# The causal mask of one-head diagonal banks: from a TensorE product to the instruction that takes the maximum

## The reference

```
scores = einsum('bhqd,bhkd->bhqk', Q, K) / sqrt(16)
scores = where(causal, scores, -100000.0)
A = softmax(scores);  Z = A V
out = sum over heads of Z WO, plus 16 * bO
```

## Time and profile before

| | us |
|---|---|
| median of three runs | 1577.11 |
| the profiled execution | 1581.26 |
| span of its trace, first to last instruction | 1579.5 |
| granted TensorE clock, mean over the span | 0.958 |
| DVE busy in the span | 1029.0 |
| attention's first unit of maxima, about | 565 to 600 |
| its steady steps, about | 600 to 1095 |

### The profile page before, as it was taken

The page is one execution under the profiler, slowest core; times in us unless marked ns, Lnnn a source line. Parts: engine busy times, 40 slices in busy tenths (PEclk is TensorE's granted clock), DMA queues, the critical chain, the costliest instruction groups (busy, mean ns, idle before and its releaser), DMA issues. The chain is left out here.

```text
span 1579.5 us, 32613 instructions
## 1 busy us (share of the span) xinstructions
PE 1429.2 (90%) x10020; PEld 978.9 (62%) x10020; DVE 1029.0 (65%) x2383; ACT 775.6 (49%) x1316; POOL 636.5 (40%) x676
## 2 busy tenths in 40 slices
PE   4899999999968879999999999999598999999997
PEld 3777888888846623443444344443276778888886
DVE  5675536365779678877788687784267564445557
ACT  4313565555125514665566466567362245655530
POOL 3371433766634460222222122222235406176764
PEclk9899999999979968999999999999879999999999
DMA  7741656887316910432224242200131227488873
GB/s 258 231 191 54 195 184 203 264 244 241 87 58 169 239 62 2 69 54 43 42 42 68 34 64 42 42 2 2 41 96 69 97 64 245 154 264 249 245 224 107
DMA packets 159219, 199.06 MB, mean 126 GB/s; under 512 B 18181, under 2 KB 132441, under 8 KB 159065
## 3 DMA queue, kind: packets, MB, share of 16 engines
q1 hardware_dynamic: 140632, 146.67, 34.9%
q0 software_dynamic: 18432, 50.36, 9.7%
HBM read 105.21 MB, written 91.49 MB: 125 GB/s over the span
## 5 line engine op out<-in xcount | busy, mean ns | idle before, releaser
L1576 ACT ACTIVATE attn_prob<-attn_b_ps 128x1024 f32<-128x1024 f32 (+3 forms) x352 | 304.1, 870 | 219.6 <-PE attn_b_ps L1744 217.7
L1622 DVE TENSOR_REDUCE attn_max_a<-attn_a_ps 128x1 f32<-128x512 f32 (+3 forms) x432 | 279.1, 669 | 72.5 <-PE attn_a_ps L1727 40.5
L475 POOL DMA_INDIRECT xs_dram<-ffn_xn,ffn_index x192 | 189.0, 984 | 229.1 <-DVE ffn_index L745 172.8
L1724 PE MATMUL attn_a_ps<-k_rows,q_rows 96*128 96x512 bf16 (+3 forms) x768 | 250.1, 348 | 21.2 <-DVEq L1614 7.5
L489 POOL DMA_INDIRECT ffn_gathered<-ys_dram,ffn_index x192 | 195.8, 1020 | 92.8 <-issue 56.0
L1520 POOL TENSOR_SCALAR_AFFINE_SELECT attn_prob<-attn_prob 128x512 f32<-128x512 f32 x128 | 81.3, 636 | 363.5 <-ACT attn_prob L1576 360.7
L789 DVE TENSOR_TENSOR ffn_xs_lo<-ffn_xt_ps,ffn_xs_hi 128x512 fp32r<-128x512 f32 x144 | 97.7, 679 | 160.1 <-ACT ffn_xs_hi L561 159.6
L1768 PE MATMUL attn_o_ps<-attn_prob,attn_v_now 128*17 128x256 f32 (+1 forms) x2560 | 187.8, 366 | 0.0
L1744 PE MATMUL attn_b_ps<-q_rows,k_rows 98*128 98x512 bf16 (+3 forms) x768 | 186.2, 330 | 0.3 <-ACT attn_prob L1576 0.3
L1724 PEld LDWEIGHTS attn_a_ps<-k_rows,q_rows 96*128 96x128 bf16 x768 | 75.0, 98 | 180.0 <-DVE attn_max_a L1622 103.2
L186 PE MATMUL ffn_gu_ps<-ffn_w_hi,ffn_xs_hi 128*128 x564 | 170.7, 303 | 2.1 <-DVE ffn_xs_lo L789 2.1
(11 more groups left out here) (196 smaller groups left out, 2691.7 us busy)
## 6 DMA issues: line engine op xcount, KB each, us to landing
ffn_xs<-xs_dram SPq DMA_DIRECT2D x138, 256.0 KB, 3.4
ys_dram<-ffn_y SPq DMA_DIRECT2D x138, 256.0 KB, 2.5
xs_dram<-ffn_y SPq DMA_DIRECT2D x16, 768.0 KB, 11.7
qk_parts<-proj_cut SPq DMA_DIRECT2D x32, 384.0 KB, 3.1
k_rows<-qk_parts SPq DMA_DIRECT2D x96, 128.0 KB, 4.5
q_rows<-qk_parts SPq DMA_DIRECT2D x96, 128.0 KB, 6.5
ffn_w_stage<-in_L_ffn_w_dram SPq DMA_DIRECT2D x64, 128.0 KB, 2.4
x_res<-in_L_attn_x_dram SPq DMA_DIRECT2D x4, 1024.0 KB, 8.3
```

Of the source, the lines that this page charges most:

```text
L475: pool.indirect_dma_start(xs_dram[(b + 1) % 2], bass.IndirectOffsetOnAxis(index[:, b, i, k:k + 1], 0), xn[:, b % 2, i, :], None, bounds_ch ...
L1576: act.activation(prob[PROB[kt]][:, h:h + heads, prob_at(kt, kt * P):prob_at(kt, S)], b_ps[:, slot, :].rearrange("p (h t) -> p h t", h=head ...
L1622: dve.tensor_reduce(dst, a_ps[:, bank, 0:heads * keys].rearrange("p (h k) -> p h k", h=heads), AX.X, ALU.max).then_inc(a_free, 1)
L1724: ins = pe.matmul(a_ps[:, bank, i * keys:end], q_rows[q][0:SROWS, h0 + i, qt * P:(qt + 1) * P], k_rows[q][0:SROWS, h0 + i, first:first + k ...
```

## The change

For diagonal banks with one head the mask product is no longer issued on PE. DVE reads the bank together with a wide mask (`mask_wide`, 512 columns of bfloat16, zero except for the triangle in the last 128) in one `tensor_tensor_reduce`: it adds the two, writes the sum to a new SBUF tile `scored` that nothing reads, and keeps the running maximum, which is put into the same place as before. Ahead of it stands a semaphore increment that carries the wait for `a_ready`. The banks with two or four heads are as before.

```diff
+        scored = sb("scored", [P, 2, HALF], BF16)
...
+        mask_qk = mask_wide[:, HALF - P:HALF]
...
             def query_maxima(item, q):
-                qt, first, keys, _, h, heads = item
+                qt, first, keys, diagonal, h, heads = item
                 bank, number = ring.take()
                 dve.wait_ge(a_ready, number + 1)
                 dst = max_b[...] if first else max_a[...]
+                if diagonal and heads == 1:
+                    dve.sem_inc(diagonal_begun, 1)
+                    dve.tensor_tensor_reduce(out=scored[:, bank, 0:keys], in0=a_ps[:, bank, 0:keys], in1=mask_wide[:, HALF - keys:HALF],
+                                             scale=1.0, scalar=NEG, op0=ALU.add, op1=ALU.max, accum_out=dst).then_inc(a_free, 1)
+                    return
                 dve.tensor_reduce(dst, a_ps[...], AX.X, ALU.max).then_inc(a_free, 1)
...
-                                    k_rows[q][0:SROWS, h0 + i, first:first + keys], start=True, stop=not diagonal)
-                    if diagonal:
-                        ins = pe.matmul(a_ps[:, bank, end - P:end], ident_b[:, :], mask_qk[:, :],
+                                    k_rows[q][0:SROWS, h0 + i, first:first + keys], start=True, stop=not (diagonal and heads > 1))
+                    if diagonal and heads > 1:
+                        ins = pe.matmul(a_ps[:, bank, end - P:end], ident_b[:, :], mask_qk,
                                         start=False, stop=True)
...
-            for t in (ident, ident_b, mask_qk):
+            for t in (ident, ident_b, mask_wide):
                 ins = pool.memset(t[:, :], 0.0)
```

More of the change, by code:

```diff
@@ L1306, in _, with attention @@
                 values(c, c % 2)
-def attention(nc, x_res, v_res, ident, ident_b, mask_qk, wo, bo, rows):
+def attention(nc, x_res, v_res, ident, ident_b, mask_wide, wo, bo, rows):
     with ExitStack() as ctx:
@@ L1362, in attention @@
         values_taken = sem("values_taken")
+        diagonal_begun = sem("diagonal_begun")
         max_ready = sem("max_ready")
@@ L1863, in _, with constants @@
             sequence(B - 1, True)
-def constants(nc, ident, ident_b, mask_qk, before_b, ones_b):
+def constants(nc, ident, ident_b, mask_wide, before_b, ones_b):
     with ExitStack() as ctx:
@@ L1884, in _ @@
                                    pattern=[[-1, P]], channel_multiplier=1).then_inc(made, 1)
-            pool.affine_select(out=mask_qk[:, :], in_=mask_qk[:, :], compare_op=ALU.is_ge, fill=NEG, base=0,
+            pool.affine_select(out=mask_wide[:, HALF - P:HALF], in_=mask_wide[:, HALF - P:HALF], compare_op=ALU.is_ge, fill=NEG, base=0,
                                pattern=[[-1, P]], channel_multiplier=1).then_inc(made, 1)
@@ L1903, in program @@
         ident_b = sb("ident_b", [P, P], BF16)
-        mask_qk = sb("mask_qk", [P, P], BF16)
+        mask_wide = sb("mask_wide", [P, HALF], BF16)
         before_b = sb("before_b", [P, P], BF16)
@@ L1908, in program @@
         row_gathered = [ctx.enter_context(nc.semaphore(f"row_gathered{i}")) for i in range(G_RING)]
-        first = constants(nc, ident, ident_b, mask_qk, before_b, ones_b)
+        first = constants(nc, ident, ident_b, mask_wide, before_b, ones_b)
         parts = nc.dram_tensor("qk_parts", [2, 3, D, TOKENS], BF16, kind="Internal").ap()
@@ L1919, in program @@
             norm_ctx.close()
-            attention(nc, x_res, v_res, ident, ident_b, mask_qk, wo, bo, rows)
+            attention(nc, x_res, v_res, ident, ident_b, mask_wide, wo, bo, rows)
         ffn(nc, "ffn2", 1, scattered, row_gathered, gate_t, None, x_res, ident, before_b, ones_b, gate_w, w1, w3, w2, xs_dram, ys_dram, out)
```

## The result

The changed kernel takes 1567.18 us (median of 9 runs, 1560.46 to 1571.9); the kernel before, run beside it, takes 1575.48 (9 runs, 1569.97 to 1580.8). The ratio is 0.9951, with a 95% interval from 0.9932 to 0.9969: 5 to 11 us faster. The forecast was 1566, a gain of 11.

The account below looks back on a forecast made before the run. PE's queue was taken to bound the kernel: -14.2 (masks removed) + 2.9 (PE waiting for DVE) + 0.35 (mask fill) = -11 us, so 1566 against the median 1577.11. Forecast's own range 1560 to 1570; 8-in-10 range 1560 to 1587.

Parts of the forecast that it names:

- What bounds it: Steady attention steps: PE's queue sets the unit's length; 236 mask products at 0.06 us each save at most 14.2 us.
- The main part of the pair: DVE's new two-operand instruction on masked banks: costs what the old reduction did, 688 ns for 512 columns.
- The half-rate rival: DVE's main part streams at half rate: about 80 us lost, 1657 in all; chance 0.04.
- The read, d: DVE's second instruction, putting out the maximum: extra time per masked bank, from 0.03 to 0.29 us, taken as 0.12.
- all rivals that rest on a long read: DVE's read of the maximum is long: Half-hidden, chance 0.28, or slower from d = 0.22 (1586 at 0.30), chance 0.18.
- The wait on its own instruction: DVE, semaphore instruction ahead of the main part: its extra step was put at 0.04 us.
- Where PE waits: Banks b7, b8 and b35: PE waits 0.14 and 0.05 us, 0.19 a unit, 2.9 us in 15 units.
- PE's growing waits: Steady attention steps, list of waits: PE's waits for DVE grow from 3 to about 6 us.
- The start: Kernel start: POOL fills 512 columns of mask instead of 128 and the other engines wait, +0.35 us.
- the first banks: 20 masked banks ahead of the steps: taken as 0 extra; about +1.5 us at d = 0.29.
- Half-hidden: Masked banks b4 to b10, b30 to b35: d 0.15 to 0.28, gain of 8 to loss of 8 us; chance 0.28.
- PE waits for something else anyway: Whole kernel: the change does nothing since PE waits for something else, 1577 us; chance 0.03.

Follow-up runs that it names:

- experiment 1: The kernel before without the mask products of one-head diagonal banks, nothing in their place, DVE unchanged; 1565.19 us, 0.9915 of the kernel before.
- experiments 3: The kernel before with only a semaphore increment, carrying the wait, ahead of the old reductions of one-head diagonal banks; 1580.24 us, 1.0016 of the kernel before.
- 4: The changed kernel with DVE's loop written out and the semaphore increment dropped, the new instruction carrying the wait; 1561.10 us, 0.9890 of the kernel before.
- experiment 5: The changed kernel with DVE's loop written out and the semaphore increment kept; 1568.40 us, 0.9945 of the kernel before.
- 10: The kernel of 4 run again, in a second set of runs; 1561.54 us, 0.9908 of the kernel before.

## Why the prediction was right

The time lies in the forecast's own range, and for the reason forecast: PE's queue gets shorter, and DVE gives nearly all banks back in time. The gain, about 8 us (5 to 11), is at the low end of the 8 to 14 that the forecast named. Two terms of it were mis-sized, in opposite directions, and that they nearly cancel is luck.

**What bounds it: right.** PE's queue sets the unit's length. Taking 16 products out of it shortened the unit by their distance, 0.06 each (0.059 by experiment 1), not by their duration of 229 ns.

**The main part of the pair: right.** Predicted as the old instruction, measured 690 and 556 ns. The half-rate rival is out by this row.

**The read, d: wrong in size.** Taken as 0.12, with 0.03 as the lowest end, below which it lies; it is 0.00 from start to start (0.61 with the read, 0.61 without). I had taken it to start when the main part is over. It starts 0.08 before that, together with the next main part. So all rivals that rest on a long read are out. "VectorE: DVE Perf Modes" of the Trainium skill was weighed there: its section "Two Vector instructions with no wait between them" agrees with these rows (0.61 between starts of instructions that last 0.69). Its section "The DRAIN you can't avoid", which the prediction set against it, itself says that a next instruction that is not held starts earlier, so the two do not disagree here.

**The wait on its own instruction: wrong in size.** Taken as 0.04 more, from the chain in the earlier trace rows; it is 0.15 (0.19 instead of 0.04), shown by experiments 3, 4 and 5. The chain's gap was that of waits which the waiting instruction itself carries, so it was no row for this. In the trace of the change the increment starts at 627.44, 0.04 after b5's product has ended, and the main part 0.15 behind the increment: the wait ends as early as before, and the step from the increment to the next instruction is what costs.

**Where PE waits: right places, near the sizes, for a wrong reason.** Predicted 0.14 at b7 and b8 and 0.05 at b35; measured 0.13 at b7 and 0.10 at b35. The free read and the dear wait nearly cancel, by luck: a bank that is waited for was to be free 0.08 + 0.75 = 0.83 after its product's end, and is free after 0.19 + 0.69 = 0.88; with the wait on the main part it would be 0.04 + 0.69 = 0.73. What I called PE's growing waits (from 3 to 6 us in that view) did not show: PE is idle 0.06 at b7 and 0.03 at b35, too short for that list, and the rest of the loss only takes overlap away.

**The start: POOL right, the first banks not quite.** 0.32 measured for 0.35. Ahead of the steps I took 0 for 20 banks and 0.4 came: a pair of masked banks takes 1.56 (first two rows) instead of 1.50. Its loop gained 0.15 of wait and lost 0.10 of mask, not 0.06: in the kernel before a bank's product runs 0.61 alone, and with its mask until 568.56, 0.71 after its start (last two rows). PE's granted clock is 0.50 in this stretch (560 to 600 after), the lower of its two levels, 1.2 of 2.4 GHz:

```profile
567.94 0.69 DVE L1627 CUSTOM_DVE_ANT_0 attn_scored<-attn_a_ps,mask_wide 128x512 bf16<-128x512 f32 x1 [0.27 <-PE attn_a_ps L1732]
...
569.50 0.69 DVE L1627 CUSTOM_DVE_ANT_0 attn_scored<-attn_a_ps,mask_wide 128x512 bf16<-128x512 f32 x1 [0.24 <-PE attn_a_ps L1732]
```

```profile
567.85 0.61 PE L1724 MATMUL attn_a_ps<-k_rows,q_rows 96*128 96x512 bf16 x1 [0.19 <-DVE attn_max_a L1622]
568.25 0.31 PE L1727 MATMUL attn_a_ps<-mask_qk,ident_b 128*128 128x128 bf16 x1
```

**The sum.** Fifteen units at 0.71 are 10.7; less 0.4 and 0.3 the change should give 10, and the measured 5 to 11 holds that. The missing 1 to 2 us of the profiled pair lie in the intervals with a seam, whose length varies between executions with the granted clock (last section); that the medians carry the same was not shown. "Half-hidden" is true of a quarter of the saving (0.23 of 0.94), not of most of it; "PE waits for something else anyway" is out.

## What to carry to other kernels

Price a small product in a busy PE queue by the distance from its start to the next start, and look for what is lost in the same distances, since a list of waits shows only idle time, and only the longer stretches of it. When an instruction cannot carry its own wait, price the instruction that carries it for it: here that step, and not the arithmetic moved to DVE, took a quarter of the gain, and giving the wait back to the instruction took the unit to the full saving. After a saving on the bounding engine the next one is near: here it was ACT, which took half of what the next 8 masks were worth.

## What the runs showed of the hardware that was not expected

- The read of DVE's accumulated maximum lasts 83 ns and starts 0.08 us before its main part ends; between back-to-back banks it takes no time of the queue (0.61 us from main part to main part).
- A semaphore increment that carries a wait ahead of a DVE instruction adds 0.11 us to the reduction's start and 0.15 to the new instruction's; the wait on the instruction itself leaves 0.04.
- At the first two seams, where its loop goes round, PE stands 2.4 to 3.2 us ("issue"; once 4.0, in experiment 5), and the granted clock afterwards differs between executions. The first bank product behind the first seam, before and then after:

```profile
751.36 0.33 PE L1724 MATMUL attn_a_ps<-k_rows,q_rows 96*128 96x384 bf16 x1 [2.49 <-issue]
```

```profile
747.98 0.50 PE L1732 MATMUL attn_a_ps<-k_rows,q_rows 96*128 96x384 bf16 x1 [2.98 <-issue]
```

The windows behind them, before and then after (columns as in the earlier trace rows):

```profile
751.00:757.00 6.00, 5.64 (x46) 2.45 (x47) 2.83 (x5) 2.11 (x3) 0.00 (x0) 0.72 0.01 4
```

```profile
749.00:755.00 6.00, 6.00 (x42) 2.06 (x41) 2.62 (x9) 2.11 (x3) 0.00 (x0) 0.52 0.00 0
```

After the change the granted clock is 0.52 there, about the lower of the two levels (1.2 of 2.4 GHz), after 2.98 us in which PE did nothing; the same product takes 0.50 us there and 0.33 at the other level. Before, the clock was low for a shorter part of the window (0.72). In experiment 1 it stayed at 1.00 behind gaps of 2.98 and 2.88 us, so the gap alone does not decide it.

Over all the traces the interval that holds such a seam lies between 37.95 and 42.41 us, while the regular units of these kernels differ by 1.6 at most. One kernel run twice (4 and 10) had 37.95 and 40.69 once, and 40.70 and 39.07 then. Their windows behind the seams, in that order:

```profile
750.20:757.00 6.80, 6.79 (x72) 2.91 (x72) 5.36 (x14) 3.35 (x5) 0.63 (x1) 1.00 0.01 2
879.80:886.60 6.80, 6.79 (x44) 2.44 (x45) 2.96 (x9) 2.11 (x3) 0.00 (x0) 0.55 0.01 2
```

```profile
744.00:750.80 6.80, 6.72 (x44) 2.36 (x45) 2.96 (x9) 2.11 (x3) 0.00 (x0) 0.54 0.01 2
876.00:882.80 6.80, 6.80 (x61) 2.69 (x62) 4.12 (x11) 2.82 (x4) 0.06 (x1) 0.75 0.01 2
```

At 1.00 the interval is 37.95, at 0.75 it is 39.07, at 0.55 and 0.54 it is 40.69 and 40.70: in this kernel the scatter of the seams goes with the granted clock. A comparison of two profiled executions carries it.
